# Layer norms behind three 16-wide cross-attentions moved into the attention loops: roots and scaling on GpSimd

## The reference, cut to what matters

```python
def _layernorm(x, axis=-1, eps=1e-05):
    m = jnp.mean(x, axis=axis, keepdims=True)
    v = jnp.var(x, axis=axis, keepdims=True)
    return (x - m) / jnp.sqrt(v + eps)
...
# behind the cross-attention of layer 0: a linear attention with a norm of its own on top
mu = jnp.mean(x, axis=-1, keepdims=True)
var = jnp.mean(jnp.square(x - mu), axis=-1, keepdims=True)
return (x - mu) * jax.lax.rsqrt(var + LN_EPS) * gamma + beta
```

## Time and profile before

| | |
|---|---|
| median of 3 runs | 2846.32 us (2844.6 to 2846.47) |
| the profiled execution, its own time | 2843.08 us |
| its span, first to last instruction | 2841.2 us |
| PE busy / PEld busy | 2468.6 us (87%) / 2089.7 us (74%) |
| DVE busy / ACT busy / POOL busy | 1713.5 us (60%) / 1398.4 us (49%) / 665.1 us (23%) |
| mean granted TensorE clock | 0.939 of full speed |

### The profile page before, as it was taken

The page is one execution under the profiler, slowest core; times in us unless marked ns, Lnnn a source line. Parts: engine busy times, 40 slices in busy tenths (PEclk is TensorE's granted clock), DMA queues, the critical chain, the costliest instruction groups (busy, mean ns, idle before and its releaser), DMA issues. The chain is left out here.

```text
span 2841.2 us, 83215 instructions
## 1 busy us (share of the span) xinstructions
PE 2468.6 (87%) x35827; PEld 2089.7 (74%) x35827; DVE 1713.5 (60%) x3397; ACT 1398.4 (49%) x3496; POOL 665.1 (23%) x862
## 2 busy tenths in 40 slices
PE   6999787999958999999997759977996766999888
PEld 5888555777746999999996548976775645999567
DVE  5777675666656433333324755657885776777663
ACT  3888424555532444444432324426884554777342
POOL 3111002212102300000000203432336535555200
PEclk9999898999988999999999859987999898999999
DMA  2110003212031100000000042332321001211100
GB/s 76 39 36 21 17 0 96 62 33 62 3 85 49 33 17 17 17 17 17 2 2 24 3 144 85 139 109 80 98 66 52 2 2 49 55 51 45 45 1 30
DMA packets 118221, 126.66 MB, mean 45 GB/s; under 512 B 10877, under 2 KB 110152, under 8 KB 117864
## 3 DMA queue, kind: packets, MB, share of 16 engines
q1 hardware_dynamic: 114024, 110.93, 12.7%
q0 software_dynamic: 3840, 10.49, 1.2%
HBM read 105.67 MB, written 15.73 MB: 43 GB/s over the span
## 5 line engine op out<-in xcount | busy, mean ns | idle before, releaser
L1030 ACT ACTIVATE s_ca_probs<-s_ca_scores,s_ca_neg_max 128x256 f32<-128x256 f32 x768 | 352.8, 477 | 35.0 <-DVE s_ca_neg_max L1074 25.5
L1074 DVE TENSOR_REDUCE s_ca_neg_max<-s_ca_scores 128x4 f32<-128x1024 f32 x192 | 234.3, 1221 | 54.5 <-PE s_ca_scores L936 27.0
L953 PE MATMUL s_ca_probs_flipped<-identity,s_ca_probs 128*128 128x128 f32 x1536 | 214.2, 284 | 11.4 <-ACT s_ca_probs L1030 10.4
L2064 DVE COPY s_mx_w_mixed<-s_mx_ps 128x512 f32<-128x512 f32 x256 | 163.7, 684 | 95.0 <-PE s_mx_ps L1910 81.5
L953 PEld LDWEIGHTS s_ca_probs_flipped<-identity,s_ca_probs 128*128 128x128 f32 x1536 | 168.1, 143 | 50.1 <-ACT s_ca_probs L1030 23.1
L2019 ACT COPY s_mx_w_mixed<-s_mx_ps 128x512 f32<-128x512 f32 x256 | 137.3, 589 | 108.1 <-PE s_mx_ps L1897 86.1
L620 PE MATMUL s_ln_flip<-identity,s_ln_xn 128*128 128x128 f32 x352 | 66.4, 372 | 108.4 <-DVE s_ln_xn L602 108.3
L1030 ACT ACTIVATION_READ_ACCUMULATOR s_ca_probs<-s_ca_scores,s_ca_neg_max 128x1 f32 x768 | 160.2, 209 | 0.0
L1037 ACT COPY s_ca_probsT<-s_ca_probs_flipped 128x512 f32<-128x512 f32 x192 | 115.1, 599 | 80.1 <-PE s_ca_probs_flipped L953 80.1
L857 POOL TENSOR_TENSOR s_ca_inv_spread<-s_ca_inv_sums,h_ca_own_half 128x128 f32<-128x128 f32 x192 | 72.6, 399 | 343.1 <-DVE s_ca_inv_sums L1096 343.1
L82 PE MATMUL s_cc_shared<-s_cc_ctxT_low,h_cc_wkv_high 128*128 128x256 f32 x512 | 146.2, 286 | 2.2 <-DVE s_cc_ctxT_low L1425 2.2
(11 more groups left out here) (513 smaller groups left out, 7374.5 us busy)
## 6 DMA issues: line engine op xcount, KB each, us to landing
h_ca_ctxT<-in_ctxT SPq DMA_DIRECT2D x96, 256.0 KB, 3.1
h_mx_w_by_input<-in_L_ffn_eW1T SPq DMA_DIRECT2D x16, 512.0 KB, 5.5
h_mx_w_by_hidden<-in_L_ffn_eW2T SPq DMA_DIRECT2D x8, 1024.0 KB
h_re_win<-in_L_ffn_W_in SPq DMA_DIRECT2D x8, 1024.0 KB, 5.9
h_ca_ctx<-in_ctx SPq DMA_DIRECT2D x32, 256.0 KB, 2.8
x_normed_transposed<-in_ctx SPq DMA_DIRECT2D x7, 1024.0 KB, 5.7
h_re_wout<-in_L_ffn_W_out SPq DMA_DIRECT2D x8, 512.0 KB, 3.9
choice_results<-s_rt_zeros SPq DMA_DIRECT2D x4, 1024.0 KB, 10.5
```

The source lines that it names most:

```text
L953: last = nc.tensor.transpose(psT[u % len(psT)][:, 2 * a + c, :], PR[b % 2][:, 4 * n + 2 * h + a, c * P:(c + 1) * P], ident[:, :])
L1030: last = nc.scalar.activation(PR[b % 2][:, p, :], psS[:, p // 2, (p % 2) * NKEY:(p % 2 + 1) * NKEY], ACT.Exp, bias=nmax[b % 2][:, p:p + 1] ...
L1074: nc.vector.tensor_reduce(nmax[b % 2][:, 4 * n:4 * n + 4], psS[:, 2 * n:2 * n + 2, :].rearrange("p r (g k) -> p r g k", g=GR), AX_X, ALU.m ...
L2064: last = nc.vector.tensor_copy(part(int(name[1]), r), bank(j, r))
```

## The change

The three `layernorm_transposed` stages behind the 16-wide cross-attentions are gone. A new class GroupNorm does their work: for 12 of the 16 tiles inside the loop of the cross-attention, for the last four at the head of the stage that consumes them. VectorE adds bn_aggr to the statistics of each tile, and after every fourth tile makes a first guess of the inverse root from the bits of the variance (3 small operations, 4 with the double norm). GpSimd refines it by three Newton steps (`refine`, batches 9, 17 and 25) and scales two tiles at a time (`normalise`, at the end of batches 10, 12, 18, 20, 26 and 28). In the batch after, TensorE transposes the pair into psO (`norm.flip`, 4 transposes, behind the first half of `flip`), ScalarE copies it to XNT (`norm.store`), and `attend` waits for that copy. The weights of the consumer are loaded at the head of the cross-attention's SyncE program, ahead of its own loads, and the splitting of layer 2's weights goes into its batches 0 and 1. Held semaphores are now put aside with the others instead of being kept to the end.

```diff
@@ held
+        sems = []
         def sem(name):
             s = nc.alloc_semaphore(unique(name))
-            kept.append(s)
+            sems.append(s)
             return s
         yield sb, sem
+    _pending.extend(sems)
@@ new class GroupNorm
+class GroupNorm:
...
+    def statistics(self, dve, i):
+        dve.bn_stats(self.ST[:, i, :], self.X[:, i, :]).then_inc(self.s_st, 1)
+        dve.wait_ge(self.s_st, i + 1)
+        dve.bn_aggr(self.MV[:, i, :], self.ST[:, i, :]).then_inc(self.s_mv, 1)
+
+    def guess(self, dve, g):
...
+        dve.wait_ge(self.s_mv, (g + 1) * self.GROUP)
+        link(dve.tensor_scalar(half[:, :, 0], self.MV[:, t, 1], 0.5, 0.5 * EPS, ALU.mult, ALU.add))
+        if n == 2:
+            link(dve.tensor_scalar(half[:, :, 1], self.MV[:, t, 1], 0.5 * (1.0 + EPS), 0.5 * EPS * EPS, ALU.mult, ALU.add))
+        link(dve.tensor_scalar(bits, half.bitcast(I32), 1, None, ALU.logical_shift_right))
+        dve.tensor_scalar(root.bitcast(I32), bits, -1.0, float(self.MAGIC), ALU.mult, ALU.add).then_inc(self.s_guess, 1)
+
+    def refine(self, pool, g):
...
+        pool.wait_ge(self.s_guess, g + 1)
+        for _ in range(self.STEPS):
+            link(pool.tensor_tensor(step, root, root, ALU.mult))
+            link(pool.tensor_tensor(step, step, half, ALU.mult))
+            link(pool.tensor_scalar(step, step, -1.0, 1.5, ALU.mult, ALU.add))
+            link(pool.tensor_tensor(root, root, step, ALU.mult))
+        if self.residual:
...
+        link(pool.tensor_tensor(shift, mean, root[:, :, self.roots - 1], ALU.mult))
+        pool.tensor_scalar(shift, shift, -1.0, 0.0, ALU.mult, ALU.add).then_inc(self.s_scale, 1)
+
+    def normalise(self, pool, u):
+        pool.wait_ge(self.s_scale, 2 * u // self.GROUP + 1)
+        if u:
+            pool.wait_ge(self.s_f, u)
+        for k in range(2):
+            i = 2 * u + k
+            last = pool.tensor_scalar(self.XN[:, k, :], self.X[:, i, :], self.root[:, i, self.roots - 1:self.roots], self.shift[:, i:i + 1],
+                                      ALU.mult, ALU.add)
+        last.then_inc(self.s_n, 1)
+        if self.residual:
...
+    def flip(self, pe, u, dst):
...
+        pe.wait_ge(self.s_n, u + 1)
+        for k in range(2):
+            for c in range(KC):
+                last = pe.transpose(dst[:, c, k, :], self.XN[:, k, c * P:(c + 1) * P], self.ident[:, :])
@@ cross_attention
+        NORM = {b: 2 * ((b - 9) // 8) + (b % 8 == 5) for b in range(9, NB) if b % 8 in (3, 5)}
...
+                for weights in loads:
+                    weights.load(sp)
+                norm.load(sp)
                 for b in range(NB):
                     load(b)
...
+                    if ahead and b < KC:
+                        ahead(pool, b)
+                    if b >= 9 and b % 8 == 1:
+                        norm.refine(pool, (b - 9) // 8)
+                    if b + 1 in NORM:
+                        norm.normalise(pool, NORM[b + 1])
...
                     flip(b, 0)
+                    if b in NORM:
+                        pe.wait_ge(s_at, b)
+                        pe.wait_ge(s_we, (b - 1) // 2)
+                        norm.flip(pe, NORM[b], psO[:, :])
...
+                    if b in NORM:
+                        pe.wait_ge(norm.s_out, NORM[b] + 1)
                     attend(b)
...
                     turned(b, 0)
+                    if b in NORM:
+                        norm.store(act, NORM[b], psO[:, :])
...
-                    nc.vector.bn_stats(ST[:, i, :], X[:, i, :])
+                    norm.statistics(dve, i)
+                    if i % 4 == 3:
+                        norm.guess(dve, i // 4)
@@ linear_attention
                 nc.gpsimd.memset(VS[:, :, P:P + 1], 1.0).then_inc(s_one, 1)
+                norm.refine(pool, 3)
+                for u in (6, 7):
+                    norm.normalise(pool, u)
...
+                dve.wait_ge(norm.s_back, TILES // 2)
                 with dve.Fori(1, LAST) as i:
@@ normed_heads
                 low(2)
+                norm.refine(pool, 3)
+                norm.normalise(pool, 6)
                 pool.wait_ge(softmax.s_w, 48)
                 for t in range(TILES):
                     normalise(t)
+                    if t == 1:
+                        norm.normalise(pool, 7)
                     if t + 3 < TILES:
                         low(t + 3)
@@ gated_recurrence
+                norm.refine(pool, 3)
+                for u in (6, 7):
+                    norm.normalise(pool, u)
                 aside.prepare(pool)
...
                 project(0, 1)
+                for u in (6, 7):
+                    norm.flip(pe, u, psG[u % 2][:, :])
+                pe.wait_ge(norm.s_out, 8)
@@ perceiver
-                layernorm_transposed(nc, X, XNT, ident, ST, twice=True, residual=True,
-                                     affine=(d["L0_attn_gamma_col"], d["L0_attn_beta_col"]), loads=(w,))
-                linear_attention(nc, X, ST, XNT, ident, w)
+                    cross_attention(nc, X, ST, QT, ident, ones, w, norm, loads=(a,))
+            linear_attention(nc, X, ST, XNT, ident, a, norm)
...
+                    cross_attention(nc, X, ST, XNT, ident, ones, w, norm, loads=(h, a, t), ahead=h.prepare)
...
+                        cross_attention(nc, X, ST, QT, ident, ones, w, norm, mask=mask4, loads=(a, f))
+                gated_recurrence(nc, X, ST, XNT, ident, a, f, norm)
```

More of the change, by code:

```diff
@@ L754, in _, with cross_attention @@
                         low_input(t + 2)
-def cross_attention(nc, X, ST, QT, ident, ones, held, mask=None):
+def cross_attention(nc, X, ST, QT, ident, ones, held, norm, mask=None, loads=(), ahead=None):
     OWN = held.OWN
@@ L1489, in _, with linear_attention @@
                 row_statistics(TILES - 1)
-def linear_attention(nc, X, ST, XNT, ident, held):
+def linear_attention(nc, X, ST, XNT, ident, held, norm):
     LAST = TILES - 1
@@ L1588, in _ @@
                 attend(0)
+                norm.flip(pe, 6, psN[:, :])
                 body(1, 0)
+                pe.wait_ge(norm.s_out, 7)
+                norm.flip(pe, 7, psN[:, :])
                 with pe.Fori(2, LAST) as i:
@@ L1617, in _ @@
                     exponentiate(i)
-                with act.Fori(1, LAST - 1) as i:
+                norm.store(act, 6, psN[:, :])
+                result(0)
+                take(3)
+                exponentiate(2)
+                norm.store(act, 7, psN[:, :])
+                act.wait_ge(norm.s_out, 8)
+                with act.Fori(2, LAST - 1) as i:
                     result(i - 1)
@@ L2556, in _, with normed_heads @@
                     nc.vector.tensor_copy(VA[:, t, :, 0:4:3, :], out[t % 4][:, 0:DIM].rearrange("p (a h d) -> p a h d", a=8, h=2)).then_inc(s_st, 1)
-def normed_heads(nc, X, XNT, QKT, VA, ident, held, softmax):
+def normed_heads(nc, X, XNT, QKT, VA, ident, held, softmax, norm):
     NX, LAG = 3, 3
@@ L2632, in _ @@
                         project(t)
+                    if t in (LAG, LAG + 2):
+                        u = 6 + (t - LAG) // 2
+                        norm.flip(pe, u, psN[u % 2][:, :])
                     if t >= LAG:
@@ L3287, in _, with gated_recurrence @@
                     nc.vector.tensor_tensor(x, psX[u % 2][:, :, :], x, ALU.add).then_inc(s_x, 1)
-def gated_recurrence(nc, X, ST, XNT, ident, held, aside):
+def gated_recurrence(nc, X, ST, XNT, ident, held, aside, norm):
     TC = 512
@@ L3374, in _ @@
                     update_gate(0, m)
+                for u in (6, 7):
+                    norm.store(act, u, psG[u % 2][:, :])
                 for t in range(NT):
@@ L3606, in perceiver @@
         mask4 = d["mask_Bx1x1xS2_fk0"].rearrange("(t b) c e s -> t b (c e s)", b=2)
-        if "L0x" in STAGES:
+        with held(nc, kept) as (sb, sem):
+            a = LinearWeights(sb, sem, d)
+            norm = GroupNorm(sb, sem, X, XNT, ident, ST, twice=True, residual=True, affine=(d["L0_attn_gamma_col"], d["L0_attn_beta_col"]))
             with held(nc, kept) as (sb, sem):
@@ L3674, in perceiver @@
-        if "L3x" in STAGES:
-            with held(nc, kept) as (sb, sem):
-                q = ProjectionWeights(sb, sem, d["L3_xattn_Wq"], d["L3_xattn_bq_col"], KC)
-                w = CrossWeights(sb, sem, d, ctx4, wkv=d["L3_xattn_Wkv"], bk=d["L3_xattn_bk_col"], bv=d["L3_xattn_bv_col"],
-                                 wo=d["L3_xattn_Wo"], bo=d["L3_xattn_bo"])
-                layernorm_transposed(nc, X, XNT, ident, ST, fresh=True, loads=(q, w))
-                with nc.sbuf_tensor("l3x_qT", [P, KC, TOKENS], F32) as QT:
-                    project_transposed(nc, XNT, QT, q, KC, aside=w)
-                    cross_attention(nc, X, ST, QT, ident, ones, w, mask=mask4)
@@ L3683, in perceiver @@
-        if "L3a" in STAGES and "L3f" in STAGES:
-            with held(nc, kept) as (sb, sem):
-                f = QuantisedWeights(sb, sem, d)
-                with held(nc, kept) as (sb, sem):
```

(15 more changed lines are left out.)

101 lines of the change are left out of this document (75 added, 26 removed).

## The result

The changed kernel took 2863.62 us (median of 16 runs, 2853.11 to 2870.17), the kernel before beside it 2848.19 us. The ratio is 1.005, 95% interval 1.0038 to 1.0061: **14 us slower** (10.8 to 17.4), where I had forecast 4.3 slower with a range up to 2865. The direction and the whole range held. The size is three times mine, and the time lies outside the 2842 to 2860 that I had given to the forecast case itself.

What follows compares the result with a forecast made beforehand. It took TensorE, busy for practically the whole length of the 16-wide loops, as the bound. Costs of 43.25 us against gains of 38.95 gave +4.3 on the median, 2850.6 us, range 2834 to 2865.

Steps and rivals of the forecast that it cites:

- the forecast case itself: Whole kernel: 4.3 us slower, 2850.6 us, own range 2842 to 2860; chance 0.50.
- The boundaries: Norm stages behind the three cross-attentions go away: gains of 14.8 us in layer 0, 13.75 in layer 2, 9.6 in layer 3.
- The transposes at 0.515 a pair: Four added TensorE transposes per pair of tiles, 18 pairs in loops without TensorE idle time: 9.3 us.
- Layer 2's wait for the scaling, 1.05 a pair: Layer 2's loop: GpSimd scales after the value copy, so TensorE stands 1.05 us in each of six pairs: 6.3 us.
- Refine's 1.2 per group: Layer 2's loop: a refine of 4.0 us makes GpSimd's inverse spread 1.2 us late, three times: 3.7 us.
- Layer 3's first mask, 7.9: Layer 3's start: the first mask waits behind 3.1 MB of weights for the next stages: 7.9 us.
- normed_heads, 5.0: Head of normed_heads: refine (4.0) and a pair (1.1) stand before GpSimd's first scaling of rows: 5.0 us, bounds 3 and 8.
- The recurrence, 2: gated_recurrence: project waits for both pairs, conversions slide into the steady loop beside VectorE: 2 us, bounds 0 and 10.
- layer 3's first pair of a group: Layer 3's loop: refine overruns GpSimd's 2.83 us idle time, mask rows and scaling come late; 1.2 us each, 3.5 in all.
- the second: Rival: GpSimd's part is hidden by its idle time, 17 us of costs against 39: 2824 to 2830 us; chance 0.13.
- The third: Rival: GpSimd and VectorE contend in the recurrence and layer 2, +8.3 us: 2858.9 us; chance 0.20.
- The first: Rival: layer 3's first mask is not held up, so the 7.9 us goes: 2842.7 us; chance 0.12.

Runs made afterwards that it cites:

- the runs with one layer: Norm inside the loop for one attention, the others with their own stage; against the kernel before: layer 0 0.9948, layer 2 1.0025, layer 3 1.0063.
- layer 0 alone: Only layer 0 has the new norm, layers 2 and 3 as in the kernel before: 0.9948 of the kernel before, -14.8 us.
- the masks ahead: Changed kernel with layer 3's later weights issued behind the loads of batches 0 to 3 (also called masks first): 1.0024 of the kernel before, 7.4 us below the changed one.
- four edits: Changed kernel with early scaling, layer 3's masks before the weights, VectorE's guess behind the reciprocal and two Newton steps: 0.993 of the kernel before, -20.0 us.
- two steps: Changed kernel with two Newton steps in place of three: 1.0013 of the kernel before, 10.5 us below the changed one.
- heads later: Changed kernel with normed_heads' refine and last two pairs moved behind the third, fourth and ninth scaling of rows: 1.0049 of the kernel before.
- the two moves: Changed kernel with pairs scaled straight behind the query spread and layer 3's masks loaded ahead of later weights, three Newton steps: 0.9968 of the kernel before, -9.1 us.
- layer 3 alone: Only layer 3 has the new norm, layers 0 and 2 as in the kernel before: 1.0063 of the kernel before, +17.9 us.
- guess behind the reciprocal: Changed kernel with VectorE's first guess moved behind the reciprocal of the sums; ran once under the profiler, no time of its own to compare.

## Why the prediction was right in direction and wrong in size

By layer, my terms against the traces and the runs with one layer:

| | my terms | two traces | alone, by the ratio |
|---|---|---|---|
| layer 0 | -10.9 | -11.6 | -14.8 |
| layer 2 | +7.4 | +7.1 | +7.1 |
| layer 3 | +7.8 | +15.2 | +17.9 |

The 16.9 that the expectations have for layer 3 counts the recurrence up to its last projection; 15.2 counts it up to its end. Layer 2's total agrees by luck: its loop cost 13.0 where my terms give 15.3, and normed_heads cost 2.4 more than I had.

- **The boundaries**: right within 0.3 us in each, tails and clearing included.
- **The transposes at 0.515 a pair**: right (0.50 to 0.53 in layer 0's batches 11 to 29). VectorE's guess, costed at 1.8 for layer 2 alone, cost 0.24 in each of layer 0's batches 9, 17 and 25 and nothing in layer 2. The splitting of weights, 0.4: nothing; batch 1 was 0.3 shorter, as in the kernel with layer 0 alone.
- **Layer 2's wait for the scaling, 1.05 a pair**: measured 1.03 to 1.06. Refine's 1.2 per group: 1.0. Refine itself, 4.0 us: 3.84 there, 4.15 in layer 3. The chain has 14 operations and not the 13 that I counted, and a link takes 0.28 and not 0.3.
- **Layer 3's first mask, 7.9**: 7.1, and 7.4 by the run with the masks ahead.
- **normed_heads, 5.0**: 7.4. The 4.9 at its head came, and 2.5 more behind it, where the second pair waits 4.28 us for TensorE and the TensorE clock is 0.86 in 2150 to 2183. In the kernel before it was 1.00 in 2160 to 2185. How much of the 2.5 is the ring and how much the clock is not shown.
- **The recurrence, 2**: 3.2 up to its last projection, of which 1.5 are left at its end (56.6 us from the first projection to the last update of x, 55.1 before). It is not from the conversions: one VectorE L3387 took 2.57 us beside them, as before, now the third and not the first, where I had named more than one as a sign. The norm stage that is gone had also let the clock rise. Its first 7 us ran at 0.52, and the first projections behind it at 1.00; now half of these run at the lower clock themselves. First the kernel before, the head of its norm stage and then its first projections; below it the first projections of the changed kernel:

```profile
2650.00:2657.00 7.00, 4.51 (x21) 4.48 (x22) 5.97 (x23) 3.94 (x7) 0.00 (x0) 0.52 0.82 266
2659.44:2664.49 5.05, 5.05 (x12) 2.37 (x13) 0.00 (x0) 1.28 (x1) 5.04 (x2) 1.00 0.19 66
```

```profile
2677.78:2684.53 6.75, 6.75 (x12) 2.96 (x13) 0.00 (x0) 1.29 (x2) 3.86 (x16) 0.75 0.00 1
```

  How much of this stretch is at the lower clock differs from profile to profile. It takes 5.1 us with four edits (clock 1.00) and 8.1 with two steps, heads later and the two moves, and the whole recurrence takes 54.9 in the first and 60.0 in the other three. A sum over one trace is uncertain by that much.

- **The step that failed is layer 3's first pair of a group**, sized at 1.2 us of wait, 3.5 us in all: it measured 11.1. Its mechanism was right as far as it went, GpSimd's refine overrunning its 2.83 us of idle time and the masks and the scaling coming late behind it. The three batches cost 4.55, 3.28 and 4.78, 12.6 together, of which 1.5 are the transposes. Three things were missing. The guess and bn_aggr stand on VectorE ahead of the reciprocal for which GpSimd waits: the reciprocal came at 5.19 instead of 4.36 us behind `attend(8)`, so GpSimd entered the group 0.83 late; with the guess moved (4.57) the wait fell by 0.44. The first scaling ran beside VectorE's L1206, 0.98 in place of 0.55. With these two the 1.2 becomes 2.46 of the 2.65. And in two of the three groups the clock fell behind the wait.

The price of the clock can be read without any model, since the same wait occurs with and without it. In the five kernels that have the wait of 2.65 or 2.69 (the changed one, layer 3 alone, masks first, heads later: twelve groups) or 2.21 (guess behind the reciprocal: three), batches with a fall cost 4.54 to 4.79 more than before and those without 3.28 to 3.31; at 2.21 it was 4.23 and 4.29 against 2.83. So a fall costs 1.2 to 1.5 us, and it came in ten of fifteen groups. At 1.63 it came in none of three, and at 1.05 in layer 2 in none.

That the range held is luck: its upper end was put at 2865 for a refine dearer than 4.0, and refine cost what I had put down. What filled it was mostly layer 3's pairs, 7.6 us above their term.

The rivals: the second (GpSimd hidden, -22) came true for layer 0 alone. The third was right in sign and near in size (2858.9), but for another place: contention and the clock met in layer 3's loop, not in the recurrence. The first was refuted by the 10.66 us of wait for the mask.

On the contention, the rows of layer 3's batch 11 tell of a two-input VectorE operation that took 1.14 us in place of 0.69 while GpSimd's scaling took 0.98 in place of 0.55, both reading from SBUF. The Trainium skill's "GPSIMD Engine Reference", section "Key points", names VectorE instructions with two SBUF inputs as such a case; these rows agree with it.

## What to carry to other kernels

When work is moved onto an engine with idle time, follow each item that waits behind it within one turn, not its busy share: in layer 2 the same 1.1 us of scaling cost a microsecond per pair behind the value copy and nothing one place earlier, and in layer 3 one place earlier still cost 0.9 in the first pair of a group, since the mask rows came behind it. List also what is put in front of the small operation on another engine that this one waits for. And count a stall in a loop in which TensorE is always busy at more than its length: the waits of 2.2 us and more here also cost the clock, in two cases of three.

## What the runs showed of the hardware that was not expected

- A TensorE wait of 2.2 to 2.7 us in the middle of a loop at full clock lowered the granted clock to 0.50 behind it in ten of fifteen cases, at 1.2 to 1.5 us each; the same wait occurs with and without the fall.
- A GpSimd row that falls beside VectorE's L1206, which reads two inputs from SBUF, took 0.3 to 0.5 us longer: the scaling 0.98 in place of 0.55, a Newton step on 128x4 0.51 in place of 0.20, and, where the scaling had been moved ahead of it, the mask's L972 1.43 in place of 0.92. L1206 itself took 1.14 in place of 0.69 in the first of these cases, where it met the mask rows as well, and 0.69 to 0.72 in the other two.
- GpSimd's operations on 128x4 and on 128x8 take the same 0.20 us, and a link with its wait 0.28 us: a chain of 14 took 3.84.
